# Attention on one core: the transposes of the score maxima and their copies stand at step 10 instead of step 9

## What is computed

```python
h = _layernorm(x, axis=-1) * (1 + ca) + sa
kqv = (h @ Wqkv + bqkv).reshape(b, s, 3, 16, 32)
scores = jnp.einsum('bsnh,btnh->bnst', k, q) / math.sqrt(32)
scores = jnp.triu(scores) + -10000.0 * jnp.tril(ones, k=-1)
attn = jax.nn.softmax(scores, axis=2)
out = jnp.einsum('bnkq,bknh->bqnh', attn, v)
x = x + ga * (out @ Wo + bo)
```

## Time and profile before

| | us |
|---|---|
| median of 3 runs (2376.22 to 2377.37) | 2376.26 |
| profiled execution | 2383.18 |
| its span | 2381.4 |
| PE busy | 1936.1 |
| DVE busy | 1152.1 |
| ACT busy | 761.1 |
| POOL busy | 610.8 |

### The profile page before, as it was taken

How to read it: one execution, slowest core, us unless ns; L and a number is a source line. 1 busy time by engine, 2 the same in 40 slices (tenths; PEclk the granted TensorE clock), 3 DMA queues, 4 the chain that set the end, 5 groups by cost and what they waited for, 6 DMA issues and landing times. The chain is left out here.

```text
span 2381.4 us, 34828 instructions
## 1 busy us (share of the span) xinstructions
PE 1936.1 (81%) x9788; PEld 1183.5 (50%) x9789; DVE 1152.1 (48%) x2951; ACT 761.1 (32%) x1215; POOL 610.8 (26%) x743
## 2 busy tenths in 40 slices
PE   4888887888887888887888876999999759999900
PEld 0644433644434544435544324767777636666600
DVE  3355544345643455633556528555555223333358
ACT  1345452245452255533344513222222112222200
POOL 0201116111125011143011144554444421000064
PEclk8889998899998899998799997999999979999955
DMA  6222203222302222312322223222222186333388
GB/s 212 54 54 54 50 23 99 53 54 54 72 5 95 54 54 54 72 46 79 64 44 43 56 92 121 97 94 93 84 84 89 66 309 229 127 128 128 113 296 309
DMA packets 104973, 232.52 MB, mean 98 GB/s; under 512 B 20440, under 2 KB 20440, under 8 KB 104812
## 3 DMA queue, kind: packets, MB, share of 16 engines
q1 hardware_dynamic: 81008, 171.86, 25.2%
q0 software_dynamic: 14848, 50.34, 5.8%
q10 hardware_dynamic: 8960, 8.41, 1.1%
HBM read 113.06 MB, written 67.17 MB: 76 GB/s over the span
## 5 line engine op out<-in xcount | busy, mean ns | idle before, releaser
L402 ACT ACTIVATE pr<-sc 128x1024 f32<-128x1024 f32 (+3 forms) x384 | 307.9, 811 | 263.2 <-PE sc L641 261.3
L661 PE MATMUL O<-pr,V 128*32 128x512 f32 (+3 forms) x3072 | 325.6, 498 | 42.6 <-ACT oD L414 42.6
L328 POOL TENSOR_SCALAR_AFFINE_SELECT pr<-pr 128x256 f32<-128x256 f32 x256 | 103.4, 409 | 969.7 <-ACT pr L402 969.7
L504 DVE TENSOR_REDUCE mx<-ring 128x1 f32<-128x512 f32 x256 | 169.6, 678 | 246.2 <-PE ring L616 244.5
L500 DVE CUSTOM_DVE_ANT_0 ring<-ring,mask 128x512 f32<-128x512 f32 (+3 forms) x512 | 240.8, 511 | 62.7 <-PE ring L616 60.4
L641 PE MATMUL sc<-stk 128*128 128x512 f32 (+3 forms) x768 | 241.6, 396 | 23.0 <-ACT pr L402 20.9
L641 PEld LDWEIGHTS sc<-stk 128*128 128x128 f32 x768 | 115.7, 189 | 262.5 <-ACT pr L402 155.3
L616 PE MATMUL ring<-stk 96*128 96x512 f32 (+3 forms) x768 | 218.0, 388 | 20.0 <-DMA stk<-st 13.1
L616 PEld LDWEIGHTS ring<-stk 96*128 96x128 f32 x768 | 144.6, 204 | 68.2 <-DVE mx L500 17.6
L529 DVE RECIPROCAL oD<-oD 128x128 f32<-128x128 f32 x128 | 117.6, 934 | 93.1 <-ACT oD L414 93.1
L1519 PE MATMUL ue<-wu_e,xT_e 128*128 x632 | 151.2, 383 | 0.1
(11 more groups left out here) (228 smaller groups left out, 3396.1 us busy)
## 6 DMA issues: line engine op xcount, KB each, us to landing
stk<-st SPq DMA_DIRECT2D x192, 256.0 KB, 5.0
x_e<-xs SPq DMA_DIRECT2D x79, 256.0 KB, 2.6
ys<-y_e SPq DMA_DIRECT2D x79, 256.0 KB, 2.0
oT<-in_L_attn_x_dram ACTq DMA_DIRECT2D x16, 512.0 KB, 5.6
st<-in_L_attn_x_dram SPq DMA_DIRECT2D x32, 256.0 KB, 3.2
x1d<-pr SPq DMA_DIRECT2D x32, 256.0 KB, 2.1
xb<-x1d SPq DMA_DIRECT2D x32, 256.0 KB, 2.9
part<-y_sh SPq DMA_DIRECT2D x32, 256.0 KB, 2.0
```

Of the source, the lines that this page charges most:

```text
L402: nc.scalar.activation(pr[:, g % PRB, :, off:], sc[g % 2][:, :, off:], ACT.Exp, scale=SCALE).then_inc(exp_done, 1)
L504: nc.vector.tensor_reduce(mx[:, heads[0]:heads[-1] + 1, qt, part], bank[:, 0:len(heads) * w].rearrange("p (e k) -> p e k", e=len(heads)), ...
L661: last = nc.tensor.matmul(O[row:row + 32, off:], V[:, col:col + DH], pr[:, g % PRB, e, off:], start=(i == 0), stop=(i == 4 * c + 3))
```

## The change

`MT_AT` is one step later. The transposes, the copies and `m_rows` of pair p+1 stand behind step 10 instead of step 9; nothing else is edited.

```diff
     NM = len(MUSES)
     M_DUE = [min(NM, -(-NM * (s + 1) // M_STEPS)) for s in range(NST)]
-    MT_AT = M_STEPS
+    MT_AT = M_STEPS + 1
     P_AT = (0, 2, 4, 6)
```

## The result

The changed kernel takes 2353.35 us (median of 5 runs, 2348.62 to 2353.90) against 2376.26 before: ratio 0.9895, interval 0.9882 to 0.9909. The medians are 22.9 us apart, 0.96%; the ratio on record is not their quotient (0.9904) and says 1.05%. Where 48 us were forecast, 23 came, and the time lies outside the range. The profiled execution took 2353.79; its span is 2352.0, and the mean granted clock over it fell from 0.922 to 0.906.

A forecast was written before the change was run, and what follows sets the result against it. TensorE bounds the kernel, standing still at pair handovers behind transposes and copies; 4 batches × (4 × 2.64 + 2 × 0.7 + 0.1) = 48 us off the median 2376.26 gives 2328, range 2316 to 2343.

The forecast's parts named there:

- The handover: From step 9's scores to the next pair's first scores: +4.97 instead of +7.61, 2.64 us gained where nothing else is late.
- The transfers as the next wait: Six SP transfers to stk for pair p+2 bind next; TensorE's waits for them go from 4 to 16.
- even handovers: Handovers out of pairs 0, 2, 4: gain 0.7 us, behind pair 2 only 0.1, because transfers land late.
- Their size: TensorE's 12 new waits for the stk transfers: 1.6 us long, 2.5 behind pair 2.
- the two signs of being wrong: Handovers out of even and odd pairs gain alike, or the sixth transfer no longer lands 5.1 us behind its issue.
- the first rival: Transfers of pair p+3 share bandwidth with p+2's last, landing 1.2 us later: 14 us less gain, 2342; chance 0.09.
- sixth transfer: Last 256 KB transfer by SP for pair p+2, taken to land as before, 5.1 us after issue, 5.8 behind pair 2.
- the rival's slower end: Transfers of pair p+3 go wholly ahead of pair p+2's last, landing 7.5 us later: 2416; chance 0.04 for slower.
- All handovers lie at 1.00 (2.4 GHz): Bound on the granted clock: handovers run at the full clock, only low stretches between them fall differently.
- 7.6 us either way: Clock bound on the total: where low stretches fall is worth 1.9 us a batch, over 4 batches.
- The rival "ScalarE": ScalarE runs late with the copies at handovers, 0.8 us visible at 16 of them: 13 us lost, 2341; chance 0.05.
- the margin of 0.7 us on the landing: In the kernel before, the sixth transfer lands at 164.8, the next pair's maxima load weights at 165.50.

The follow-up runs named there:

- e4: The changed kernel with SP holding the transfers of pair p+3 until the next pair's second scores are done: 2347.74 us, ratio 0.9868.
- e1: The changed kernel with eight unneeded matmuls filling TensorE's wait for the transfers in step 0 of the odd pairs: 2330.84 us, ratio 0.9802.
- e5: The kernel before with P_AT = (0, 2, 4, 8), the last projection two steps later, which puts a stall into the old order: 2445.84 us, ratio 1.0294.
- e9: The kernel before with P_AT = (0, 2, 4, 8) and eleven unneeded matmuls filling the stall: 2414.67 us, ratio 1.0158.
- e6: The changed kernel with the maxima spread over steps 1 to 8 and their wait for the transfers in step 1: 2329.78 us, ratio 0.9800.

## Why the prediction was wrong, point by point

- **The handover** was right. From step 9's scores to the next pair's first scores it took 4.97 to 4.98 us at all 28, where it had taken 7.61 to 7.62. Where no stall stands, the pairs are shorter by it: pairs 2 and 4 took 35.43 us in the mean instead of 38.06, pair 6 24.8 instead of 27.4, and the wait before the transposes shrank from 1.25 to 0.45, as written.
- **The transfers as the next wait** were right: 12 new waits at the even handovers and none elsewhere.
- **Their size** was somewhat low. I took the landing as unmoved; it came 0.37 us later in the mean, most of it by the followers (e4). This was one of the two signs of being wrong that the prediction had named. That is the first rival at less than a third of its price, 4 us of 14. I had argued against it from a sixth transfer "with none close behind it"; in truth the first follower was issued 1.0 to 1.9 us before the landing even in the kernel before, and 3.1 to 4.4 before it now. The queue kept its order, and the rival's slower end did not show.
- **The step that failed** is the bound written as "All handovers lie at 1.00 (2.4 GHz)", by which the sum had no term for the clock behind the new stalls. That was the clock of the old handovers, whose idle time came as three gaps of 1.25, 0.96 and 0.75. I had myself computed a single gap of 1.6 to 2.5 us for 12 of the new ones, and charged for it only its length. The clock fell there 11 times and took 12 × (26.66 − 24.73) = 23 us with it (e1), and e5 and e9 show the same in the old order. I looked for the clock's price only between batches, as 7.6 us either way; it is a term of its own in the sum: 48 − 23 − 4 = 21, measured 23.
- **The rival "ScalarE"** did not occur: the next pair's first scores stood at +4.97 in every handover. Its time, 2341, and the first rival's, 2342, lay nearer to the result than mine, but by luck: most of the loss has the clock for its cause, which neither names.
- With the stall filled, the kernel takes 2330.84 us, the forecast's 2328 and the late landings: the sum of the order was right to 3 us.

## What to carry to other kernels

When an edit closes small gaps and the work then meets one later wait, price that wait twice: its length, and what TensorE's clock costs behind it. The sum by stretches with the granted clock shows it at once, as equal work of unequal length. Before moving a consumer earlier, move its producer too: here the margin of 0.7 us on the landing told that the later step alone could have only part of its gain, and one number in the projections' places gave most of the rest. If a wait can't be removed, matmuls that nobody needs, in a bank about to be overwritten, were worth 22.5 us.

## What I had not expected of the hardware

Stalls of 1.85 to 3.13 us in otherwise busy TensorE work were followed by a fall of the granted clock to 0.50 in 11 of 12 cases, 3.4 to 10.2 us long, while the old handovers, with 2.96 us idle in three gaps within 7.17 us, had none in 28. The length of the stall alone does not decide: one of 1.88 us had no fall, and in e6 one of 1.20 had one and one of 1.70 had none. In e4 one of 1.60 had a fall and one of 1.96 had none. What decides between these I could not tell from the traces. The Trainium skill, TensorE: Matmul & The Clock Gate, section "What's actually happening", says that the throttled state is the default and activity releases it; the traces agree as far as that filling the stall kept the clock at 1.00 in all 24 cases (e1, e9).
